# The last down product of each network part taken by pieces of the gated vector, and layer 0's shared network split three to one

## The chip, the cores and the metric

The kernel runs on one core of one Trainium2 chip. The metric is the device time of one execution in microseconds (us), the median of several runs. The five engines are called PE (TensorE), DVE (VectorE), ACT (ScalarE), POOL (GpSimd) and SP (SyncE, which here only issues transfers). Each runs its own queue in order; they wait for one another by semaphores.

## The reference, cut to what matters

Four layers act on x (2 x 1024 tokens of 256 features, float32). Each adds to x a conditioning step followed by a network step:

```python
x = x + _L0_ffn_ref(_L0_cond_ref(x, cond_1024, ...), ...)   # 32 experts, top 1, and a shared network
x = x + _L1_ffn_ref(_L1_cond_ref(x, cond_1024, mask, ...), ...)
x = x + _L2_ffn_ref(_L2_cond_ref(x, cond_1024, ...), ...)   # 8 experts, top 2, and shared networks, twice
x = x + _L3_ffn_ref(_L3_cond_ref(x, cond_1024, ...), ...)   # 8 experts, top 2, shared; then 16 experts with a capacity
```

In the parts that matter here every token goes through a shared gated network and, beside it, through the experts that a router picks:

```python
shared = (silu(x @ gate) * (x @ up)) @ down        # 256 -> 512 -> 256, one or two such units
out    = shared + sum(gates[:, e] * expert_e(x) for the picked e)
```

## The kernel before, in words

**Jobs, pieces, products.** The shared networks are class `Glu`. A job is a pair (unit of weights, chunk of 512 tokens); there are four chunks. The hidden vector of 512 numbers is cut into NF = 4 pieces of 128. `up_part(m)` makes the gate and the up product of piece m % 4 of job m // 4: 12 matmuls of 128x512, as each float32 product is three float32r ones (`matmul_split`, L315 to L322; all matmuls of the shared networks have the lines L320, L321 and L322). ACT takes the silu (L474), DVE multiplies by the up product (`multiply`, L499), ACT copies the high part of the result (`hidden_high`, L481) and DVE subtracts it to give the low part (`hidden_low`, L505), which counts the semaphore `hidden`. `down(n)` then makes the 512x256 result of job n: two halves of 256 tokens, in PSUM banks 6 and 7, each of two groups q of 128 tokens, each group a sum over the four pieces f, so 2 x 2 x 4 x 3 = 48 matmuls of 128x256. It waits once for all four pieces of the job, and for each half until DVE's `add` has taken that bank's previous result. After each half it counts `downed`; `add(n)` takes each half with one DVE instruction (L1498, L1636, L1637 or L1773, by part).

**Order.** `pe_jobs` issues the four up parts of job n + 1, then `down(n)`; for the last job of a call no up parts follow. `dve_jobs` does for each piece m: `multiply(m)`, `hidden_low(m - 1)`, and behind the multiplication of a job's last piece the `add` of the job before and what is given as `between` (`mix`, which adds the gathered expert rows of a chunk; 8 DVE instructions of 128x256 on L1749 or L1882, or one of 128x1024 on L1612 in layer 0). So the `hidden_low` of the very last piece stands behind that `add` and that `mix`.

**Front and behind.** Each of the four network parts (`half_l0`, `half_cond(2)`, `half_ffn2`, `half_cond(3)`) calls `pe_jobs` twice: for the first `split` jobs ahead of the expert stage (the front), with the remaining ones behind it. The fronts cover the routing and the gathering of rows, the part behind covers the loads of the experts' results. Splits are 2 of 4 jobs in layer 0, 4 of 8 in both parts of layer 2, 3 of 4 in layer 3's. At the end PE turns the chunks into feature order (`turn_result`, L447), copied by ACT.

**Layer 0's experts** (`LaneExperts`) run 24 rounds of four lanes. Their weights come through a ring in order of expert, issued by SP (L1051); ACT and DVE copy each round's weights into `own` (L1078), three regions of which lie over the split space of the shared network. `wait_space` says when these are free: the gate weights' region behind all up parts of the front, the up weights' region behind the down product of the job before the front's last.

**Places.** A router's decision becomes row numbers in `Slots`. PE's `pe_places` (L1279 to L1285) waits for a DVE scan (L1272) and is followed on DVE by `places` (L1292 to L1308); only behind this does DVE reach `multiply(0)`. `up_part(3)` and later ones wait until `multiply` has freed the PSUM banks of part m - 3. PE issues up parts 0 and 1 ahead of `pe_places`, 2 and 3 behind it.

Of the kernel before, what the change touches and what calls it, by code (L numbers as in the profile page):

```python
# [23 lines left out]
P = 128  # L24
B, S, D = 2, 1024, 256
T = B * S
NT = T // P
KD = D // P
CH = 512
NCH = T // CH  # L30
TPC = CH // P
TPB = S // P
FU = 512
# [16 lines left out]
def build(nc, a, out):  # L50
    ctx = ExitStack()
    with ctx:
# [263 lines left out]
        def matmul_split(pe, to, w, x, start, stop):  # L316

            pe.matmul(to, w[0], x[0], start=start, stop=False)  # L320
            pe.matmul(to, w[0], x[1], start=False, stop=False)  # L321
            return pe.matmul(to, w[1], x[0], start=False, stop=stop)  # L322
# [56 lines left out]
        class Glu:  # L379
# [42 lines left out]
            def down(self, pe, n):  # L422
# [6 lines left out]
                for half in range(2):  # L429
# [8 lines left out]
                                                f == 0, f == self.NF - 1)  # L438
                    last.then_inc(self.downed, 1)

            def turn_result(self, pe, tok, c, count):

                if count:
                    pe.wait_ge(self.featured, 2 * count)
                for k in range(KD):
                    for q in range(TPC):
                        last = pe.transpose(psum[:, 6 + k, q * P:(q + 1) * P], tok[:, c * TPC + q, k * P:(k + 1) * P], ident[:])  # L447
                    last.then_inc(self.turned, 1)
                self.await_featured = 2 * (count + 1)
# [63 lines left out]
            def pe_jobs(self, pe, n0, n1, first=True, between=None, places=None):  # L513

                if first:
                    for f in range(self.NF):
                        self.up_part(pe, self.NF * n0 + f)
                for n in range(n0, n1):
                    for f in range(self.NF if n + 1 < n1 else 0):
                        self.up_part(pe, self.NF * (n + 1) + f)  # L520
                        if f == 1 and between is not None and n > n0:
                            between(n - 1)
                        if f == 2 and places is not None and n == n0:
                            places.pe_trace(pe)
                    if places is not None and n == n0:
                        places.wait_rows(pe)
                    self.down(pe, n)

            def act_jobs(self, act, n0, n1, between=None):

# [484 lines left out]
        class LaneExperts:  # L1015


            def __init__(self, tag, on, halves, lanes, weights, region_up, region_down, space, rows, slots, glu, hT):

                self.halves, self.lanes, self.weights, self.rows, self.rounds = halves, lanes, weights, rows, rows.tiles  # L1020
                self.tile_expert, self.last_round = slots.tile_expert, slots.last_tile
                self.NE, self.NF, self.F, self.W = weights.shape[0], halves * FU // P, halves * FU, P // lanes
                self.KF, self.FD = KD * self.F, self.NF * D
                self.ring_up = region_up.rearrange("p (r n) -> p r n", r=lanes)
                self.ring_down = region_down.rearrange("p (r n) -> p r n", r=lanes)
                self.own = [space[:, n * lanes * self.KF:(n + 1) * lanes * self.KF].rearrange("p (g n) -> p g n", g=lanes)
                            for n in range(3)]
                self.sg, self.h, self.hT = glu.sg, glu.product, hT
                self.rT = sb(tag + "_rT", [P, 2, KD, P], on=on)
                self.up_in = [sem(f"{tag}_up_in{r}") for r in range(2)]  # L1030
                self.down_in = [sem(f"{tag}_down_in{r}") for r in range(2)]
                self.act_own = [sem(f"{tag}_act_own{n}") for n in range(3)]
                self.dve_own = [sem(f"{tag}_dve_own{n}") for n in range(3)]
                self.rows_t, self.rows_c, self.gate, self.silud, self.up = (
                    sem(f"{tag}_{n}") for n in ("rows_t", "rows_c", "gate", "silud", "up"))
                self.hidden, self.hid_t, self.hid_c, self.downed, self.outc = (
                    sem(f"{tag}_{n}") for n in ("hidden", "hid_t", "hid_c", "downed", "outc"))
# [449 lines left out]
        def half_l0():  # L1487


            with ExitStack() as own:  # L1490
                jobs, split = [(0, 0), (0, 1), (0, 2), (0, 3)], 2
                order, written, scaled, mixed = (sem("h0_" + n) for n in ("order", "written", "scaled", "mixed"))
                got = [sem(f"h0_got{c}") for c in range(NCH)]

# [17 lines left out]
                with nc.Block() as block:  # L1512
                    @block.sync
                    def _(sp):
                        def ready(sp):
                            for c in range(NCH):
                                sp.wait_ge(scaled, c + 1)
                                sp.dma_start(chunk_of(by_token, c), ctok[:, c * TPC:(c + 1) * TPC, :]).then_inc(written, 16)
                            places.wait_known(sp)
                            sp.wait_ge(written, 16 * NCH)  # L1520
                        experts.load_weights(sp, ready)
                        line.wait_stored(sp)
                        for c in (2, 3, 0, 1):
                            load_results(sp, [ctok], c, got[c])
                        sp.dma_start(l1_weights, a["l1_w"]).then_inc(l1_in, 16)
                        sp.dma_start(l1_words[:, 0:TPB, :], a["mask_words"].rearrange("(i p) s -> p i s", p=P)
                                     ).then_inc(l1_mask, 16)
                        sp.dma_start(l1_words[:, TPB, :], a["mask_words"][0, :].partition_broadcast(P)).then_inc(l1_mask, 16)
                        sp.wait_ge(glu.wsplit, 6)
                        sp.dma_start(wbuf[:], unit_data["g2a"]).then_inc(unit_in["g2a"], 16)  # L1530
# [13 lines left out]
                    @block.tensor  # L1544
                    def _(pe):
                        route.pe_logits(pe)
                        route.pe_turn(pe)
                        for m in range(2):
                            glu.up_part(pe, m)
                        places.pe_places(pe)  # L1550
                        for m in range(2, 4):
                            glu.up_part(pe, m)
                        glu.pe_jobs(pe, 0, split, first=False, places=places)
                        pe.wait_ge(glu.added, 2 * split)
                        experts.pe_tiles(pe)
                        glu.pe_jobs(pe, split, NCH)
                        for count, c in enumerate((2, 3, 0, 1)):
                            pe.wait_ge(glu.added, 2 * NCH)
                            pe.wait_ge(mixed, count + 1)
                            glu.turn_result(pe, xtok, c, count)  # L1560

                    @block.scalar
                    def _(act):
                        glu.features_high(act, 0)
                        for q in range(4):
                            glu.weights_high(act, 0, q)
                        route.act_quads(act)
                        for q in range(4, 6):
                            glu.weights_high(act, 0, q)
                        route.act_score(act)  # L1570
                        glu.act_jobs(act, 0, split)
                        places.wait_known(act)
                        first = experts.act_open(act, wait_space)
                        act.wait_ge(glu.downed, 2 * split)
                        experts.act_tiles(act, first)
                        act.wait_ge(experts.hidden, experts.rounds)
                        act.wait_ge(experts.downed, experts.rounds)
                        glu.features_high(act, split)
                        glu.act_jobs(act, split, NCH)
                        for count, c in enumerate((2, 3, 0, 1)):  # L1580
                            glu.copy_result(act, fx, c, count)

                    @block.vector
                    def _(dve):
# [29 lines left out]
                            dve.wait_ge(mixed, count + 1)  # L1614

                        glu.dve_jobs(dve, split, NCH, lambda n: mix(jobs[n][1], n - split))
                        mix(0, 2)
                        mix(1, 3)

        def half_cond(n, wr, bias, units, jobs, split, experts_w, scale, after):  # L1620

# [139 lines left out]
        def half_ffn2():  # L1761


            with ExitStack() as own:
# [22 lines left out]
                with nc.Block() as block:  # L1787
# [23 lines left out]
                    def _(pe):  # L1811
                        route.pe_logits(pe)
                        route.pe_turn(pe)
                        for m in range(2):
                            glu.up_part(pe, m)
                        places.pe_places(pe)
                        for m in range(2, 4):
                            glu.up_part(pe, m)
                        glu.pe_jobs(pe, 0, split, first=False, places=places)
                        pe.wait_ge(glu.added, 2 * split)  # L1820
                        experts.pe_tiles(pe)
# [1309 lines left out]
```

## Time and profile before

| | us |
|---|---|
| median of 3 runs (1671.03 to 1673.64) | 1671.27 |
| the profiled execution, its own time | 1685.24 |
| span of its instructions | 1683.5 |
| PE busy | 1471.8 |
| DVE busy | 984.0 |
| ACT busy | 656.8 |
| POOL busy | 428.6 |

The mean granted TensorE clock of the execution is 0.931 of full speed. The profiled execution took 14.0 us longer than the median of the runs. Times in rows are from the span's start. A timeline row ends with the idle time ahead of it and what released it.

### The profile page before, as it was taken

To read this page: it belongs to the slowest core of one execution; us is meant where nothing else is said; L and a number is where in the kernel's file an instruction comes from. 1 tells how busy PE (TensorE), PEld (TensorE's weight loads), DVE (VectorE), ACT (ScalarE), POOL (GpSimd) and SP (SyncE) were. 2 spreads that over 40 slices of the span, in tenths; PEclk is the share of its full clock that TensorE was granted. 3 is DMA by queue.
4 is the path that set the end of the run, shared out by engine and by line. 5 is a ranking of instruction groups with operands and counts; after the bars stand their busy time and mean duration, and the time that the engine had idled before them with its cause. 6 is when DMAs were issued, how large, how long until landed. Compare 5 with 4: busy or idle time off the path is not lost. (4 is left out here: it accounts for less than half of the span.)

```text
span 1683.5 us, 25908 instructions
## 1 busy us (share of the span) xinstructions
PE 1471.8 (87%) x8350; PEld 1117.3 (66%) x8350; DVE 984.0 (58%) x1754; ACT 656.8 (39%) x977; POOL 428.6 (25%) x366
## 2 busy tenths in 40 slices
PE   7886888765989998798999999999979899759994
PEld 5632334733877787687888888887867777636663
DVE  5665676335644364735777776775646333447665
ACT  3366775213233332424655555553332233211110
POOL 0612231000433410010233443332004334113331
PEclk9999999955899999999999999999998999859997
DMA  5378972252222240240221322201313222355743
GB/s 178 110 289 323 335 250 100 99 195 101 88 100 88 92 153 1 88 175 4 98 101 31 113 86 104 100 23 33 121 33 117 101 86 91 119 209 166 251 147 122
DMA packets 82918, 211.38 MB, mean 126 GB/s; under 512 B 10785, under 2 KB 57762, under 8 KB 74594
## 3 DMA queue, kind: packets, MB, share of 16 engines
q1 hardware_dynamic: 66944, 166.40, 27.6%
q0 software_dynamic: 15840, 43.27, 7.7%
q8 instruction: 76, 1.25, 0.3%
q14 instruction: 56, 0.46, 0.1%
q10 hardware_dynamic: 2, 0.00, 0.0%
HBM read 165.21 MB, written 44.43 MB: 125 GB/s over the span
## 5 line engine op out<-in xcount | busy, mean ns | idle before, releaser
L633 POOL DMA_INDIRECT results<-sb_big,sb_s_out_row x63 | 134.2, 2130 | 452.8 <-ACT sb_big L864 298.1
L938 DVE TENSOR_TENSOR sb_h_split<-sb_big,sb_h_split 128x2048 fp32r<-128x2048 f32 x78 | 178.5, 2289 | 87.1 <-ACT sb_h_split L933 87.1
L933 ACT CAST sb_h_split<-sb_big 128x2048 fp32r x78 | 146.6, 1903 | 34.2 <-issue 32.9
L829 PE MATMUL ps<-sb_big,sb_e_hT 128*128 x624 | 141.0, 379 | 1.1 <-DVE sb_e_hT L986 1.1
L1078 ACT COPY sb_g_space<-sb_big 128x1024 f32 x120 | 118.7, 1050 | 47.5 <-DMA sb_big<-in_l_routed 23.5
L320 PE MATMUL ps<-sb_h_split 128*128 128x512 f32 x312 | 133.1, 426 | 3.8 <-issue 2.8
L1078 DVE COPY sb_g_space<-sb_big 128x1024 f32 x168 | 108.1, 698 | 47.3 <-DMA sb_big<-in_l_routed 21.8
L829 PEld LDWEIGHTS ps<-sb_big,sb_e_hT 128*128 128x128 f32 x624 | 118.2, 190 | 18.5 <-issue 1.3
L1479 POOL DMA_INDIRECT sorted_in<-sb_big,sb_p_slots x64 | 70.2, 1097 | 222.7 <-DVE sb_p_slots L1304 167.4
L322 PE MATMUL ps<-sb_h_split 128*128 128x512 f32 x312 | 123.9, 397 | 0.0
L321 PE MATMUL ps<-sb_h_split 128*128 128x512 f32 x312 | 123.6, 396 | 0.0
L320 PE MATMUL ps<-sb_g_split,sb_g_ws 128*128 128x512 f32 x256 | 107.0, 418 | 13.0 <-DVE sb_g_product L499 8.0
L595 POOL DMA_INDIRECT results<-sb_big,sb_p_out_row x78 | 76.6, 982 | 139.6 <-DVE sb_big L744 139.0
L1116 PE MATMUL ps<-sb_g_space,sb_e_rT 128*32 128x512 f32 x768 | 94.9, 611 | 19.4 <-issue 11.3
L321 PE MATMUL ps<-sb_g_split,sb_g_ws 128*128 128x512 f32 x256 | 104.0, 406 | 0.3 <-issue 0.3
L322 PE MATMUL ps<-sb_g_split,sb_g_ws 128*128 128x512 f32 x256 | 103.4, 404 | 0.0
L622 POOL DMA_INDIRECT sb_big<-by_token,sb_s_in_row x63 | 63.6, 1010 | 145.8 <-DVE sb_s_out_row L1352 127.2
L320 PE MATMUL ps<-sb_g_ws,sb_g_split 128*128 128x256 f32 x256 | 77.4, 303 | 22.9 <-DVE sb_g_split L505 21.3
L474 ACT ACTIVATE sb_g_sg<-ps 128x512 f32<-128x512 f32 x64 | 38.1, 597 | 145.6 <-PE ps L322 136.2
L676 PE MATMUL ps<-sb_big,sb_x_rT 128*128 x312 | 87.5, 403 | 4.2 <-ACT sb_x_rT L721 4.0
L499 DVE TENSOR_TENSOR sb_g_product<-sb_g_sg,ps 128x512 f32<-128x512 f32 x64 | 43.8, 685 | 67.5 <-ACT sb_g_sg L474 59.1
L696 PE MATMUL ps<-sb_big,sb_x_hT 128*128 x312 | 81.8, 385 | 0.0
(450 smaller groups left out, 3193.3 us busy)
## 6 DMA issues: line engine op xcount, KB each, us to landing
sb_big<-in_l_routed SPq DMA_DIRECT2D x32, 1024.0 KB
sb_big<-in_l2f_routed SPq DMA_DIRECT2D x8, 3072.0 KB, 10.6
sb_e_wring<-in_l_experts SPq DMA_DIRECT2D x16, 1408.0 KB
sb_big<-in_l_routed SPq DMA_DIRECT2D x32, 512.0 KB
sb_big<-results SPq DMA_DIRECT2D x32, 512.0 KB, 7.5
sb_big<-sorted_in SPq DMA_DIRECT2D x18, 512.0 KB
by_token<-sb_big SPq DMA_DIRECT2D x12, 512.0 KB, 4.2
sorted_in<-sb_l1p_zero SPq DMA_DIRECT2D x2, 2048.0 KB, 9.6
```

Of the source, the lines that this page charges most:

```text
L320: pe.matmul(to, w[0], x[0], start=start, stop=False)
L321: pe.matmul(to, w[0], x[1], start=False, stop=False)
L322: return pe.matmul(to, w[1], x[0], start=False, stop=stop)
L595: pool.indirect_dma_start(out=results, out_offset=bass.IndirectOffsetOnAxis(ap=places.out_row[:, j:j + 1], axis=0), in_=self.tile(j), in_o ...
L633: pool.indirect_dma_start(out=results, out_offset=bass.IndirectOffsetOnAxis(ap=places.out_row[:, j:j + 1], axis=0), in_=self.tile(j), in_o ...
L676: last = pe.matmul(psum[:, j % 2, 0:self.NF * P], self.rT[:, j % 2, k * P:(k + 1) * P], self.w[:, e, k * self.NF * P:(k + 1) * self.NF * P ...
L696: last = pe.matmul(psum[:, 2 + j % 2, 0:D], self.hT[:, j % 2, f * P:(f + 1) * P], self.w[:, e, lo:lo + D].rearrange("p s n -> p (s n)"), s ...
L829: last = pe.matmul(psum[:, 7, 0:D], self.hT[:, f // TPC, f % TPC * P:(f % TPC + 1) * P], self.weight(place, 2 * KD * self.F + f * D, D), s ...
L933: act.copy(self.own[part][:, 0, :], self.raw(e, part)).then_inc(self.own_high[part], 1)
L938: dve.tensor_tensor(self.own[part][:, 1, :], self.raw(e, part), self.own[part][:, 0, :], ALU.subtract).then_inc(self.own_low[part], 1)
L1078: last = copy(self.own[part][:, g, :], here.rearrange("p s n -> p (s n)"))
L1116: last = pe.matmul(psum[g * W:(g + 1) * W, 2 * part + u % 2, :], self.rT[:, r % 2, k, g * W:(g + 1) * W], self.own[part][:, g, lo:lo + FU] ...
```

## The change

The last job of each call of `pe_jobs` uses a new function in which the pieces f are the outer loop: the product for all four groups of 128 tokens is made for piece 0, then for piece 1, and so on, each waiting for its own piece only; both banks must have been taken by `add` at the start. In layer 0 the split is 3 instead of 2, with the chunks' order behind the experts and the regions of `own` changed to match. In `half_ffn2` alone `pe_places` stands behind three up parts instead of two.

```diff
+            def down_by_hidden(self, pe, n):
+                unit = self.jobs[n][0]
+                if n == 0 or self.jobs[n - 1][0] != unit:
+                    pe.wait_ge(self.wsplit, 6 * unit + 6)
+                if self.await_featured:
+                    pe.wait_ge(self.featured, self.await_featured)
+                if n >= 1:
+                    pe.wait_ge(self.added, 2 * n)
+                for f in range(self.NF):
+                    pe.wait_ge(self.hidden, self.NF * n + f + 1)
+                    for half in range(2):
+                        for q in range(2):
+                            t0, lo = (2 * half + q) * P, 2 * KD * FU + f * D
+                            last = matmul_split(pe, psum[:, 6 + half, q * D:(q + 1) * D],
+                                                [self.hs[:, n % 2, part, f, t0:t0 + P] for part in range(2)],
+                                                [self.ws[:, part, lo:lo + D] for part in range(2)],
+                                                f == 0 and q == 0, f == self.NF - 1 and q == 1)
+                        if f == self.NF - 1:
+                            last.then_inc(self.downed, 1)
@@ pe_jobs
-                    self.down(pe, n)
+                    if n + 1 == n1:
+                        self.down_by_hidden(pe, n)
+                    else:
+                        self.down(pe, n)
@@ LaneExperts
-                            for n in range(3)]
+                            for n in (0, 2, 1)]
@@ half_l0
-                jobs, split = [(0, 0), (0, 1), (0, 2), (0, 3)], 2
+                jobs, split = [(0, c) for c in range(NCH)], 3
+                chunk_order = tuple(range(split, NCH)) + tuple(range(split))
-                        for c in (2, 3, 0, 1):
+                        for c in chunk_order:
                             load_results(sp, [ctok], c, got[c])
-                        for count, c in enumerate((2, 3, 0, 1)):
+                        for count, c in enumerate(chunk_order):
-                        mix(0, 2)
-                        mix(1, 3)
+                        for c in range(split):
+                            mix(c, NCH - split + c)
@@ half_ffn2, tensor
-                        for m in range(2):
+                        for m in range(3):
                             glu.up_part(pe, m)
                         places.pe_places(pe)
-                        for m in range(2, 4):
-                            glu.up_part(pe, m)
+                        glu.up_part(pe, 3)
```

## Rows read from the trace of the kernel before

**Rows 1.** The page: busy time, share of the span and instructions of each engine.

```profile
PE 1471.8 (87%) x8350; PEld 1117.3 (66%) x8350; DVE 984.0 (58%) x1754; ACT 656.8 (39%) x977; POOL 428.6 (25%) x366
```

**Rows 2.** PE's timeline, first matmul of a last down: start, duration, [idle before <-releaser].

```profile
78.66 0.58 PE L320 MATMUL ps<-sb_g_ws,sb_g_split 128*128 128x256 f32 x1 [5.52 <-DVE sb_g_split L505]
314.78 0.58 PE L320 MATMUL ps<-sb_g_ws,sb_g_split 128*128 128x256 f32 x1 [2.64 <-DVE sb_g_split L505]
494.27 0.39 PE L320 MATMUL ps<-sb_g_ws,sb_g_split 128*128 128x256 f32 x1 [1.38 <-DVE sb_g_split L505]
664.01 0.58 PE L320 MATMUL ps<-sb_g_ws,sb_g_split 128*128 128x256 f32 x1 [4.80 <-DVE sb_g_split L505]
1455.76 0.58 PE L320 MATMUL ps<-sb_g_ws,sb_g_split 128*128 128x256 f32 x1 [5.50 <-DVE sb_g_split L505]
```

**Rows 3.** Stretches (last downs): us, busy (x) of PE, PEld, DVE, ACT, POOL, PEclk, DMA, GB/s.

```profile
79.04:82.24 3.20, 3.20 (x16) 3.20 (x16) 2.21 (x4) 0.37 (x1) 0.00 (x0) 0.50 0.02 5
494.27:500.29 6.02, 6.01 (x48) 5.81 (x48) 0.69 (x1) 0.00 (x0) 0.00 (x0) 1.00 0.54 178
664.01:672.27 8.26, 8.26 (x48) 8.26 (x48) 0.69 (x1) 0.00 (x0) 0.00 (x0) 0.65 0.00 0
1243.67:1250.96 7.29, 7.29 (x48) 7.08 (x48) 0.69 (x1) 0.00 (x0) 0.00 (x0) 0.80 0.00 0
1455.76:1464.33 8.57, 8.56 (x48) 8.36 (x48) 0.69 (x1) 0.00 (x0) 0.00 (x0) 0.66 0.02 7
```

**Rows 4.** Timeline of DVE, end of layer 2's conditioning part.

```profile
659.25 0.69 DVE L1637 SCALAR_TENSOR_TENSOR sb_big<-ps,sb_big 128x512 f32<-128x512 f32 x1 [2.18 <-PE ps L322]
659.86 3.37 DVE L1749 SCALAR_TENSOR_TENSOR sb_big<-sb_big,sb_t_gates 128x256 f32<-128x256 f32 x8
663.26 0.69 DVE L505 TENSOR_TENSOR sb_g_split<-sb_g_product,sb_g_split 128x512 fp32r<-128x512 f32 x1
```

**Rows 5.** Timeline of DVE, the front of layer 2's conditioning part.

```profile
492.92 0.69 DVE L1636 TENSOR_SCALAR sb_big<-ps 128x512 f32<-128x512 f32 x1 [2.18 <-PE ps L322]
```

**Rows 6.** Timeline of DVE, layer 3's network part behind its experts.

```profile
1451.53 0.68 DVE L505 TENSOR_TENSOR sb_g_split<-sb_g_product,sb_g_split 128x512 fp32r<-128x512 f32 x1
1455.01 0.69 DVE L505 TENSOR_TENSOR sb_g_split<-sb_g_product,sb_g_split 128x512 fp32r<-128x512 f32 x1
```

**Rows 7.** Timeline of DVE and PE, the end of `half_ffn2`'s front.

```profile
768.88 1.28 DVE L1773 SCALAR_TENSOR_TENSOR sb_big<-ps,sb_big 128x512 f32<-128x512 f32 x2
770.21 0.44 PE L946 MATMUL ps<-sb_ident,sb_big 128*128 128x128 f32 x2 [1.55 <-DVE sb_big L1773]
```

**Rows 8.** Timeline of PE and DVE, the front of layer 0.

```profile
72.86 0.28 PE L322 MATMUL ps<-sb_g_ws,sb_g_split 128*128 128x256 f32 x1
77.31 0.69 DVE L1498 TENSOR_TENSOR sb_big<-ps,sb_big 128x512 f32<-128x512 f32 x1 [6.32 <-remote]
87.18 0.44 PE L1100 MATMUL ps<-sb_ident,sb_big 128*128 128x128 f32 x2 [0.78 <-DVE sb_big L1498]
```

**Rows 9.** Stretches: four up parts (`half_ffn2`); layer 0's network behind its experts.

```profile
744.44:755.35 10.91, 10.91 (x51) 9.02 (x49) 4.56 (x7) 3.32 (x6) 0.00 (x0) 1.00 0.01 2
282.74:323.05 40.31, 36.89 (x193) 32.23 (x193) 16.63 (x24) 8.96 (x16) 0.00 (x0) 0.92 0.44 160
```

**Rows 10.** Stretches: layer 0's first rounds, behind its experts, layer 3's last down.

```profile
88.00:92.00 4.00, 3.86 (x34) 1.04 (x34) 1.30 (x2) 1.39 (x4) 0.00 (x0) 1.00 0.03 10
304.00:308.00 4.00, 4.00 (x26) 3.61 (x25) 2.23 (x4) 2.14 (x5) 0.00 (x0) 1.00 0.00 0
1456.00:1460.00 4.00, 4.00 (x20) 4.00 (x21) 0.00 (x0) 0.00 (x0) 0.00 (x0) 0.50 0.02 6
```

**Rows 11.** PE's timeline about the places of `half_ffn2`.

```profile
689.08 0.39 PE L1279 MATMUL ps<-sb_r_work,sb_ones 128*128 128x8 f32 x2 [1.34 <-DVE sb_r_work L1272]
698.45 0.47 PE L320 MATMUL ps<-sb_h_split,sb_h_ws 128*128 128x512 f32 x1 [1.74 <-DVE sb_h_product L499]
```

**Rows 12.** PE's timeline, layer 0's first expert round.

```profile
88.14 1.92 PE L1116 MATMUL ps<-sb_g_space,sb_e_rT 128*32 128x512 f32 x16 [0.52 <-ACT sb_e_rT L1170]
```

More of the change, by code:

```diff
@@ L1579, in _ @@
                         glu.act_jobs(act, split, NCH)
-                        for count, c in enumerate((2, 3, 0, 1)):
+                        for count, c in enumerate(chunk_order):
                             glu.copy_result(act, fx, c, count)
```

## The prediction

> **What bounds the kernel now.** First the busy times on the page: PE is busy for 1471.8 us, DVE for 984.0 [rows 1], so PE is the engine to read and its idle 212 us are what can go without less arithmetic. Then PE's timeline, looked through for idle time above 1.2 us. All eight last down products have it, always released by L505, the low part of the last piece: 5.52 and 2.64 us in layer 0, 1.38 in the front of layer 2's conditioning part (the fronts of `half_ffn2` and layer 3 repeat this to 0.13 us), 4.80 behind its experts (`half_ffn2` repeats it, 4.79), 5.50 in layer 3 [rows 2]. Together 27.5 us. Then the granted clock over these products: behind 1.38 us of idleness 48 matmuls took 6.02 us at clock 1.00 (the 2.4 GHz level); behind 4.8 us they took 8.26 and 7.29 us at 0.65 and 0.80, behind 5.50 us 8.57 us at 0.66 [rows 3]. So a wait is paid for twice, as idle time and as a product part of which runs at the lower level (1.2 GHz). Last DVE's order: in layer 2 the add of the job before starts at 659.25, the mix takes 3.37 us, and only then comes L505 [rows 4].
>
> **Waits after the change.** The new product needs only both adds to begin; its pieces 0 to 2 are long ready. 36 of 48 matmuls are 36/48 x 6.02 = 4.5 us, and the last 12 take 1.5. From DVE's end to PE's start is 0.06 us (663.26 + 0.69 to 664.01) [rows 2, 4]. The four extra semaphore waits I cost at nothing, as they are fulfilled when PE comes to them; were each 0.06 us it would be 0.2 us a product, 2 in all.
>
> *Layer 2 behind the experts of the conditioning part.* The add ends at 659.94, PE starts at 660.00 instead of 664.01. The mix and L505 end at 663.95, ahead of piece 3 at 664.5, so nothing waits: 4.01 us. The gap left is about 0.8 us, less than the 1.38 that left the clock at 1.00 [rows 2, 3], so I take 6.02 for the product instead of 8.26: 2.24 more. Bounds of this clock term 0 and 2.24. Sum -6.25.
>
> *`half_ffn2` behind its experts.* Same mechanism, same 3.4 us of mix: -4.0 and -(7.29 - 6.02) = -1.27 [rows 3]. Sum -5.27.
>
> *Fronts of the conditioning parts.* No mix stands there, only L505: the add at 492.92 ends at 493.61, PE can start at 493.67 instead of 494.27 [rows 2, 5]: -0.60 each, -1.20 for two.
>
> *Front of `half_ffn2`.* Again 0.6 us earlier, but PE's next instruction waits for the last adds, which on DVE stand behind the copies of the first experts' weights: they run from 768.88 to 770.16 while the down product is over at 768.66, and PE starts at 770.21 [rows 7]. 0; bounds 0 and -0.6.
>
> *Layer 3 behind its experts.* Only one job is there, so no add holds PE. Pieces 0 and 1 follow the up parts at about 1450.3 and last 3.0 us; piece 2's low part is ready at 1452.21, before they end; piece 3's at 1455.70 [rows 6]. PE idles some 1 us, starts the last 12 at 1455.76 and ends at 1457.3 instead of 1464.33 [rows 3]: -7.0. The results for the mixes that follow must have landed: transfers are over by 1456 [rows 10], the next mix starts at 1458. If the clock still fell in the 1 us gap, the last 12 would take 2.6: +1.1.
>
> **Layer 0.** *Front.* Down(0) has its last matmul at 72.86 [rows 8] and matmul starts are 0.12 us apart (6.02/48 less the tail), so it ends at 72.98. Old: DVE got word of it only at 77.31, released by "remote" [rows 8], a lateness of 4.3 us while POOL's gathers ran; the last down follows at 78.66, the experts start at 87.18. New: job 2's up parts follow down(0) at once and hide the lateness: 10.91 us by the stretch of four up parts [rows 9] to 83.9, down(1) 5.8 to 89.7, add to 90.45, last down 90.5 to 96.5, adds 0.8, experts at 97.3. That is +10.1. *Behind.* Old 40.31 us from the first up part to the first turn [rows 9]. New: four up parts and one down less a wait. The 40.31 are 8 up parts, 5.9, 2.64, 7.49 and 0.8, so the up parts took 23.5; four of them at 10.91 drop out, 12.6 stay; 6.0 and 0.8 follow: 19.4. The mix there is one instruction of 1.2 us, and the low part of piece 3 comes within the 4.5 us of the first three. -20.9. Net -10.8. If the lateness were not in an execution at all, the old front would be at 81.2 and the net -4.8; both are bounds. What hides the moved job's other work: its features, silu, multiply and split run on ACT and DVE beside PE's up parts as for the other jobs; SP's queue loses nothing, POOL's gathers are issued at the same time. SP's weight ring restarts when the copies into `own` are made, about 2.3 us nearer to PE's start than now; the transfers almost stand still from 88 to 92 [rows 10], which hides that; uncovered it would cost 2.3. Behind, the transfers of results, layer 1's weights and mask are over by 304 [rows 10] and layer 1 needs them some 21 us earlier than at 332, at 311: 7 us to spare. The changed order of `own` costs nothing, as each region is free before its copy starts.
>
> **The places of `half_ffn2`.** Here I expect a loss. PE waits 1.34 us for the scan, from 687.74 to 689.08 [rows 11]. The third up part takes 10.91/4 = 2.73, to 690.47, so the places come 1.4 us later. DVE waits for them and then works without a pause to the multiplications for which PE waits at 698.45 [rows 11]; PE's time saved there is idle anyway. +1.4; bounds 0 (if DVE's chain had slack) and +2.7 (a whole part).
>
> **Sum.** -10.8 - 6.25 - 5.27 - 1.20 + 0 - 7.0 + 1.4 = -29.1 against the profiled execution's own 1685.24 (span 1683.5 and 1.7 around it): 1656.1. The runs' median is 14.0 us lower, so some stretches seen here, the lateness perhaps among them, are not in every execution. I take half of the 6.0 between the bounds of layer 0: -26, from 1671.27 to 1645.
>
> **A rule against the change.** In an expert round 16 matmuls go in turn to four quarters of PSUM in 1.92 us at clock 1.00 [rows 10, 12], 0.12 each, so going to and fro costs nothing there. The Trainium skill, TensorE: Matmul & The Clock Gate, section "A second HAM failure mode: psum-queue depth-cycling", says that cycling through banks can leave PE with small pauses between groups, enough for the clock to oscillate; the new product changes bank every 6 matmuls and the old one once. By that rule the last products would all run at the lower level, the third rival below; by the row they would not.
>
> **The rivals.**
> 1. *The clock isn't won and the lateness isn't there.* The waits go, but products stay as slow as in rows 3 and layer 0 gives 4.8. For: the clock may respond to more than the gap just before. Against: the 1.38 us gap left it at 1.00. -26 + 3 + (2.24 + 1.27 + 1.1) = -18, 1653.
> 2. *All of it.* The lateness is in the timed runs too and is hidden: -29, 1642; further waits of that kind vanishing could bring some us more.
> 3. *Slower: the product by pieces runs at half pace.* Starts 0.213 us apart at clock 0.50 (15 in 3.20 us) [rows 3] instead of 0.12: 10.2 us a product instead of 6.0, eight times, two of these microseconds hidden in `half_ffn2`'s front: +32. With -26 it is +6, 1677. It decides from 26/8 = 3.3 us a product, 0.07 a matmul. Against it: the expert rounds.
> 4. *No change: the time comes back.* Layer 0's experts are paced by the weight stream and later copies cost what the front's lateness gives, and behind them and in layer 3 the result transfers, not PE, end last. Layer 0 would give 0 and layer 3 some 2 of 7; with the places at +2.7 and the clock terms at 0 some -9 remain, 1662; less than 3 us is left only if layer 2 loses half as well. Against: the idle transfer engines of rows 10.
>
> **How the numbers follow.** Forecast 0.60 (its own range 1641 to 1650), rival 1 0.17, rival 2 0.11, rival 3 0.05, rival 4 0.07, of which 0.04 end within 0.2%. The range 1637 to 1656 holds the forecast and the first two. 0.2% is 3.3 us, about what a measurement of this kernel can tell from no change. Faster 0.90, same 0.04, slower 0.06.
>
> **What would show it.** Right: no idle time above 1.2 us ahead of the last downs, clock 1.00 in them, the product in layer 3 pausing before its last 12 matmuls only; layer 0's experts starting near 97 and the first turn there some 11 us earlier than 323; in `half_ffn2` L1279 1.4 us later after the second up part and the next parts later by as much. Wrong: last downs longer than 6.2 us; a shorter way through the places; an expert stage in layer 0 longer than the present 193 us; PE waiting for a transfer at the start of layer 1.

## The result, and the profile after

| | before | after |
|---|---|---|
| median (us) | 1672.45 (1671.03 to 1673.74, 4 runs) | 1648.46 (1646.90 to 1651.50, 4 runs) |
| profiled execution, its own time | 1685.24 | 1651.50 |
| span, mean granted clock | 1683.5, 0.931 | 1649.8, 0.934 |

The ratio is 0.9859, with a 95% interval of 0.9841 to 0.9877: 24.0 us faster. The profiled executions differ by 33.7 us, more than the medians; where the difference comes from is told below. In the kernel after, L447 has become L468, L474 L495, L499 L520, L505 L526, L1078 L1102, L1279 L1303, L1498 L1523, L1636 and L1637 L1661 and L1662, L1749 L1774, L2874 L2898.

The page of the kernel after, busy times:

```profile
PE 1462.4 (89%) x8350; PEld 1109.7 (67%) x8350; DVE 983.9 (60%) x1754; ACT 657.0 (40%) x977; POOL 428.0 (26%) x366
```

The same instructions are there as in [rows 1]. PE is busy 9.4 us less, as more of its work runs at the higher level of the clock (mean 0.934 against 0.931), and its idle time in the span falls from 211.7 to 187.4 us.

PE's timeline after, at the last downs, as in [rows 2]: the front and behind in layer 0, the front and behind in layer 2's conditioning part, behind in `half_ffn2`, and in layer 3 the first matmul of the last piece:

```profile
92.60 0.39 PE L320 MATMUL ps<-sb_g_ws,sb_g_split 128*128 128x256 f32 x1 [0.79 <-DVE sb_big L1523]
305.96 0.28 PE L320 MATMUL ps<-sb_g_ws,sb_g_split 128*128 128x256 f32 x1
482.45 0.39 PE L320 MATMUL ps<-sb_g_ws,sb_g_split 128*128 128x256 f32 x1 [0.78 <-DVE sb_big L1661]
648.22 0.36 PE L320 MATMUL ps<-sb_g_ws,sb_g_split 128*128 128x256 f32 x1 [0.83 <-issue]
1222.54 0.35 PE L320 MATMUL ps<-sb_h_ws,sb_h_split 128*128 128x256 f32 x1 [0.83 <-issue]
1423.46 0.39 PE L320 MATMUL ps<-sb_g_ws,sb_g_split 128*128 128x256 f32 x1 [1.19 <-DVE sb_g_split L526]
```

Where a job stands before the last one, 0.78 to 0.83 us of idle time remain. The releaser is now the `add` in the fronts; behind the experts of layer 2 the trace names none ("issue"), but in the conditioning part the `add`, shown below, ends 0.10 us before PE's start. Behind layer 0's experts the job is alone, and PE doesn't pause. The low part L526 releases PE once, in layer 3, 1.19 us ahead of the last 12 matmuls. Windows over these products, to set against [rows 3] (us, busy (x) of PE, PEld, DVE, ACT, POOL, PEclk, DMA, GB/s):

```profile
92.60:98.61 6.01, 6.01 (x48) 5.80 (x48) 3.72 (x6) 1.35 (x2) 0.00 (x0) 1.00 0.12 19
648.22:654.21 5.99, 5.99 (x48) 5.79 (x48) 4.52 (x10) 0.00 (x0) 0.00 (x0) 1.00 0.01 1
1222.54:1228.51 5.97, 5.97 (x48) 5.77 (x48) 4.52 (x10) 0.00 (x0) 0.00 (x0) 1.00 0.00 0
1417.80:1425.16 7.36, 6.17 (x49) 5.76 (x47) 5.39 (x12) 1.73 (x3) 0.00 (x0) 1.00 0.83 264
```

All have clock 1.00 and 0.12 us a matmul. In [rows 3] the first had 0.50 in the stretch shown, the others 0.65, 0.80 and 0.66. DVE, at the end of layer 2's conditioning part, to set against [rows 4]; the mix of L1774 now lies beside PE's product instead of ahead of it:

```profile
647.43 0.69 DVE L1662 SCALAR_TENSOR_TENSOR sb_big<-ps,sb_big 128x512 f32<-128x512 f32 x1 [2.18 <-PE ps L322]
```

**Stage by stage.** Distances in us between landmarks in the traces. "Behind" runs from the first matmul of the last group of expert products to the next stage's first matmul, layer 3's front from the rows' trace (L1338 before) to the first expert product, and the last row from the first expert product to the last. "places" is the kernel before with only the places moved; it and the two others stand here because they ran beside kernels before that took 1672 to 1673 us, near the median, and not 1685 as the profiled execution did.

| stretch | before | places | after | after again (e9) | pieces alone (e10) |
|---|---|---|---|---|---|
| layer 0, start to first expert product | 88.1 | 83.3 | 100.4 | 99.8 | 83.1 |
| its expert products | 188.6 | 189.5 | 186.4 | 188.8 | 185.0 |
| their end to layer 1 | 55.5 | 54.0 | 35.0 | 33.2 | 50.9 |
| sum to layer 1 | 332.2 | 326.8 | 321.8 | 321.8 | 319.0 |
| layer 1 | 72.5 | 72.8 | 73.0 | 72.8 | 71.3 |
| behind, layer 2 conditioning | 83.7 | 82.6 | 77.2 | 77.2 | 77.2 |
| `half_ffn2`, start to places | 11.8 | 14.6 | 13.0 | 14.6 | 11.8 |
| behind, `half_ffn2` | 89.6 | 90.8 | 84.3 | 84.3 | 84.4 |
| front, layer 3 conditioning | 55.2 | 46.5 | 45.9 | 45.9 | 45.9 |
| behind, layer 3 conditioning | 41.7 | 40.6 | 34.9 | 34.8 | 34.9 |
| layer 3's last expert products | 152.2 | 153.7 | 156.8 | 153.6 | 156.7 |

Layer 1 is in the table because no edit touches it: over all fourteen traces it takes from 68.3 us (e6, mean granted clock 0.63) to 73.1 (e11, 0.55). Differences of that size between two single traces can come without any change.

### The profile page after: what moved, and what is told of

Read it like the earlier page. It is cut to its first block and busy times, and to the rows that moved or that the text cites. A ratio compares the mean times of both kernels' runs of the same rounds, so it can differ in the third digit from the quotient of the medians.

```text
span 1649.8 us, 25908 instructions
## 1 busy us (share of the span) xinstructions
PE 1462.4 (89%) x8350; PEld 1109.7 (67%) x8350; DVE 983.9 (60%) x1754; ACT 657.0 (40%) x977; POOL 428.0 (26%) x366
## 5 line engine op out<-in xcount | busy, mean ns | idle before, releaser
L1102 DVE COPY sb_g_space<-sb_big 128x1024 f32 x168 | 107.9, 698 | 48.8 <-DMA sb_big<-in_l_routed 23.2
L1102 ACT COPY sb_g_space<-sb_big 128x1024 f32 x120 | 118.5, 1046 | 40.7 <-DMA sb_big<-in_l_routed 21.7
L495 ACT ACTIVATE sb_g_sg<-ps 128x512 f32<-128x512 f32 x64 | 38.1, 597 | 143.5 <-PE ps L322 143.3
L520 DVE TENSOR_TENSOR sb_g_product<-sb_g_sg,ps 128x512 f32<-128x512 f32 x64 | 43.9, 685 | 74.1 <-ACT sb_g_sg L495 73.1
L2898 PE MATMUL ps<-sb_e_wring,sb_e_rT 128*128 x124 | 66.6, 662 | 11.6 <-issue 5.1
```

What stands on the lines that cost most here:

```text
L1102: last = copy(self.own[part][:, g, :], here.rearrange("p s n -> p (s n)"))
L2898: last = pe.matmul(psum[:, j % 2, :], rT[:, j % 2, k * P:(k + 1) * P], wring[:, place, k * FU:(k + 1) * FU].rearrange("p s n -> p (s n)"), ...
```

## The experiments

The kernels ran in three groups of four, each group beside its own runs of the kernel before. Those had medians of 1671.81 us (first group, 23 runs), 1687.21 (second, 11 runs) and 1673.34 (third, 11 runs), so ratios and not times are compared between groups. The record gives each group a chip of its own, so group and chip can't be told apart here. One run of 23 in the first group's kernel before (1771.07 us) and one of 12 in e3's (3800.73) stand far outside; the medians don't depend on them.

**e1: the product by pieces alone.** The change without its edits of the split and of the places.

```diff
-                jobs, split = [(0, c) for c in range(NCH)], 3
+                jobs, split = [(0, c) for c in range(NCH)], 2
-                        for m in range(3):
+                        for m in range(2):
```

> Only the last down products by pieces, in all four network parts; layer 0 split 2 to 2 and the places as before. Theory (wait and clock, place by place from the two traces): -6.3 in layer 2's conditioning part, -5.3 in its network part, -7.0 in layer 3, -0.6 in each of two fronts, and in layer 0 without the split some -0.6 in front and -3 behind (2.64 us of waiting less 0.8, and a product at full clock): about -23 us. Rival (most of the gain is the layer 0 split, the rest comes back): -12 us or less.

Measured: 1646.30 (1643.30 to 1647.77), ratio 0.9848 [0.9823, 0.9873], 25.5 us less. I expected some 23. The product by pieces brings all that the whole change brought (24.0).

**e2: the split alone.** The split of three to one with the old `down` and the old places.

```diff
-                    if n + 1 == n1:
-                        self.down_by_hidden(pe, n)
-                    else:
-                        self.down(pe, n)
+                    self.down(pe, n)
```

> Only layer 0's split 3 to 1, with its chunk order and its copies' regions; all down products as before. Theory: three jobs in front hide the late word of down(0), but the last downs keep their own wait for L505 (1.4 us in front; behind, with a single job, some 4 us at the lower clock): -10.8 less what the pieces give there, so -3 to -7 us if the lateness is in the timed runs, about 0 if it is a thing of the profiled execution only. Rival (the split alone makes the gain of 10): -10 us.

Measured: 1669.28, ratio 0.9986 [0.9970, 1.0002]: 2.5 us less, which the interval does not tell from nothing. In its trace the part up to layer 1 takes 325.1 us, where "places", which has the old layer 0, has 326.8. The last down behind layer 0's experts still waits for the low part, and runs below full clock (PE's timeline, then a window):

```profile
307.62 0.38 PE L320 MATMUL ps<-sb_g_ws,sb_g_split 128*128 128x256 f32 x1 [3.87 <-DVE sb_g_split L526]
```

```profile
307.62:315.00 7.38, 7.38 (x48) 7.29 (x48) 0.69 (x1) 0.00 (x0) 0.00 (x0) 0.77 0.29 120
```

A job that is alone behind the experts has its mix ahead of its last low part, too: the split moves work, but not the wait.

**e3: the places alone.**

```diff
-                        for m in range(2):
+                        for m in range(3):
                             glu.up_part(pe, m)
                         places.pe_places(pe)
-                        for m in range(2, 4):
-                            glu.up_part(pe, m)
+                        glu.up_part(pe, 3)
```

> Only half_ffn2's places behind three up parts instead of two. Theory: DVE's chain from the scan's count to the multiplications sets the end there, so the part is 1.1 to 1.4 us slower: +1.2 us in all. Rival (PE is the bound and gains the moved part's time): -1 to -3 us.

Measured: 1672.64 (all but one run 1666.35 to 1676.34), ratio 1.0006 [0.9987, 1.0025], not resolved in time. The trace shows the loss where it was looked for: `half_ffn2` reaches the places 14.6 us from its start instead of 11.8, and from there to the rows' trace takes 19.7 in place of 19.8. Three up parts stand ahead of the places (windows over those 36 matmuls, first e3, then the kernel after):

```profile
674.38:684.23 9.85, 9.85 (x36) 8.01 (x37) 5.74 (x18) 4.91 (x6) 0.00 (x0) 0.83 0.25 82
```

```profile
663.69:671.99 8.30, 8.30 (x36) 6.87 (x37) 5.75 (x18) 4.92 (x6) 0.00 (x0) 1.00 0.29 98
```

The same 36 matmuls cost 9.85 us at clock 0.83 and 8.30 at 1.00, and e9, the same kernel as the one after, has 9.90 at 0.83. So the move costs 1.2 us or 2.8, as the clock happens to be.

**e4: the change with the old places.** The kernel after, with `range(2)` and the two remaining up parts behind the places.

```diff
-                        for m in range(3):
+                        for m in range(2):
```

> The changed kernel with half_ffn2's places back behind two up parts. Theory: 1.2 us faster than the changed kernel, so some 25 us below the kernel before. Rival (the third up part belongs ahead of the places): 1 to 3 us slower than the changed kernel.

Measured: 1646.78 (1642.03 to 1651.25), ratio 0.9850 [0.9823, 0.9876]. It is beside e1 (0.5 us apart), so with the pieces in, three to one and two to two are the same there. Against the kernel after (0.9859, another group) a gain from the old places of 1 to 3 us is not excluded and not shown by the times.

**e5: keep PE busy in the gaps.** The kernel before, with matmuls whose results nobody reads in the gaps behind the experts. Nothing ends earlier on DVE.

```diff
+                self.warm = {'g0': 20, 'g2': 36, 'h2': 36, 'g3': 40}[tag]
+                if warm:
+                    m = self.NF * (n + 1) - 2
+                    pe.wait_ge(self.multiplied, m + 1)
+                    for _ in range(warm):
+                        pe.matmul(psum[:, m % 3 * 2, 0:D], self.ws[:, 0, 0:P], self.ws[:, 0, 0:D], start=True, stop=True)
```

> The kernel before with matmuls of no use (20, 36, 36 and 40, each 128x256, result thrown away in a free PSUM bank) in PE's wait ahead of the last down product behind the experts, in layer 0, both parts of layer 2, and layer 3. Waits stay as they are; only the idleness goes. Theory (a gap costs twice, the product behind it runs partly at 1.2 GHz): the four products take 6.0 us instead of 7.5, 8.3, 7.3 and 8.6, so -7 us. Rival (the lower clock comes from something other than the gap): products as long as before, 0 or slightly slower.

Measured: 1672.84 beside 1687.21, ratio 0.9916 [0.9886, 0.9946], 14.4 us less (9 to 19). Windows over the four products behind the experts:

```profile
314.30:320.33 6.03, 6.01 (x48) 5.81 (x48) 0.69 (x1) 0.00 (x0) 0.00 (x0) 1.00 0.00 0
661.70:667.70 6.00, 5.98 (x48) 5.77 (x48) 0.69 (x1) 0.00 (x0) 0.00 (x0) 1.00 0.01 3
1238.80:1244.80 6.00, 5.95 (x48) 5.82 (x48) 0.69 (x1) 0.00 (x0) 0.00 (x0) 1.00 0.01 3
1449.60:1455.60 6.00, 5.97 (x48) 5.81 (x48) 0.69 (x1) 0.00 (x0) 0.00 (x0) 1.00 0.04 15
```

The real matmuls are the same and wait for the same low part as before, and they take 6.0 us instead of 7.5, 8.5, 7.3 and 8.6 (the second from its start to the end of its last matmul, 0.24 us more than the stretch in [rows 3]):

```profile
664.01:672.51 8.50, 8.50 (x48) 8.30 (x48) 0.69 (x1) 0.00 (x0) 0.00 (x0) 0.66 0.00 0
```

So the idle stretch itself lowered the clock, and that is worth 7.8 us by these four alone, where 7 were expected. The stretches of the table that hold them (to layer 1, and the three behind) are shorter than before's by 1.9, 2.5, 1.3 and 2.6 us, 8.3 in sum, and the two profiled executions differ by as much (1685.24 and 1676.72). The medians differ by 14.4, and by 9 at the least; what is above 8.3 isn't placed.

**e6: the low part first.** The kernel before with one DVE instruction moved: the low part of a call's very last piece is made ahead of the `add` and the mix. The product stays whole.

```diff
+                    if m == self.NF * n1 - 1:
+                        self.hidden_low(dve, m)
@@ behind the loop
-                self.hidden_low(dve, self.NF * n1 - 1)
```

> The kernel before with one change on DVE: the low part of the last piece (L505) right behind the piece's multiplication, ahead of the add of the job before and of the mix; products in the old order. Theory (DVE's order made the wait, the order of the product only hides it): PE goes from one down product to the next without a wait in layer 2 and the fronts, and waits some 2.7 us in layer 3; -25 us in all, as much as the pieces give. Rival (the pieces themselves are needed): -8 us or less.

Measured: 1657.51 beside 1687.21, ratio 0.9829 [0.9798, 0.9859], 29.7 us less, where I expected 25: as much as the product by pieces (0.9848 and 0.9853). DVE's timeline behind layer 2's conditioning part: two low parts together, then the two adds, then the first of the mix:

```profile
641.59 1.46 DVE L505 TENSOR_TENSOR sb_g_split<-sb_g_product,sb_g_split 128x512 fp32r<-128x512 f32 x2
643.23 0.69 DVE L1638 SCALAR_TENSOR_TENSOR sb_big<-ps,sb_big 128x512 f32<-128x512 f32 x1 [0.18 <-PE ps L322]
646.11 0.69 DVE L1638 SCALAR_TENSOR_TENSOR sb_big<-ps,sb_big 128x512 f32<-128x512 f32 x1 [2.19 <-PE ps L322]
646.72 0.47 DVE L1750 SCALAR_TENSOR_TENSOR sb_big<-sb_big,sb_t_gates 128x256 f32<-128x256 f32 x1
```

PE has no idle time at all ahead of this last down. In layer 0's front 2.06 us remain, released by the `add`. A wait for the low part is left only where a job is alone, in layer 3, since the up parts end 2.8 us ahead of it:

```profile
1426.93 0.39 PE L320 MATMUL ps<-sb_g_ws,sb_g_split 128*128 128x256 f32 x1 [2.79 <-DVE sb_g_split L505]
```

The product behind this pause runs at full clock all the same (window over it):

```profile
1426.93:1432.95 6.02, 6.01 (x48) 5.81 (x48) 3.36 (x9) 0.00 (x0) 0.00 (x0) 1.00 0.51 160
```

The waits of [rows 2] thus came from DVE's order, and either side can take them away: PE asks for less at a time, or DVE does the awaited part first.

**e7 and e8: both together, split two and three.** Low part first, and the product half by half with piece 3 last; a job that is alone goes piece by piece. e8 has layer 0's three to one, both have the old places. The core of e7, then what e8 changes (with it the regions of `own`, as in the change):

```diff
+                order = [(f, half) for half in range(2) for f in range(self.NF - 1)]
+                if alone:
+                    order = sorted(order)
+                seen = set()
+                for f, half in order + [(self.NF - 1, 0), (self.NF - 1, 1)]:
+                    if f == 0 and n >= 1:
+                        pe.wait_ge(self.added, 2 * (n - 1) + half + 1)
...
-                jobs, split = [(0, c) for c in range(NCH)], 2
+                jobs, split = [(0, c) for c in range(NCH)], 3
```

> Layer 0 split 2 to 2, places as before, the last down by pieces, and two things more: its pieces 0 to 2 are made half by half, so that the first half waits for its own bank's add only, and DVE makes the last low part ahead of add and mix. Theory: the remaining waits of 0.8 us (four of them) and the 1.2 us in layer 3 go: 4 us faster than the product by pieces alone, -29 us against the kernel before. Rival (these waits are hidden behind DVE, whose add and mix still have to follow): as the pieces alone, -25 us.

> As e7_halves_low, with layer 0's split of 3 to 1. Theory from the first four runs (with the pieces the split is worth about nothing): within 1 us of e7_halves_low. Rival (three jobs in front still help by the wait behind the experts): 2 us faster than it.

Measured: e7 1658.46, ratio 0.9833 [0.9803, 0.9864]; e8 1651.16, ratio 0.9797 [0.9767, 0.9826]. Beside e6 (0.9829) e7 shows no gain at all, where 4 us over the pieces alone were expected: with a split of two to two, both edits together give no more than either. In their traces e7 is 2.0 us shorter than e6 up to layer 1 and 2.8 behind in layer 3's conditioning part, but 4.5 longer in layer 1, which has the same code in both.

Three to one took 7.3 us more off the median, where I expected at most 1. The traces differ by as much (spans 1656.7 and 1649.4), but hardly where the edit is: up to layer 1 e7 takes 323.5 us and e8 323.0. Of the rest 1.9 lie in layer 1 and 2.6 behind layer 3's conditioning part, the others in pieces of under 1, all in equal code. In both, `add` in a front gets word of PE late, as in [rows 8]. DVE's timeline of e8:

```profile
468.20 0.69 DVE L1670 TENSOR_SCALAR sb_big<-ps 128x512 f32<-128x512 f32 x1 [5.07 <-remote]
```

**e9 to e12: the four against one another.** All beside a kernel before of 1673.34. e9 is the change again, e10 is e1's code, e11 is e8's. e12 is e8 with the plain product:

```diff
-                    if n + 1 == n1:
-                        self.down_by_hidden(pe, n, n == n0)
-                    else:
-                        self.down(pe, n)
+                    self.down(pe, n)
```

> The changed kernel again, beside the others on one chip, to see how its gain differs by chip. Theory (the late words of down products are a property of the chip, and layer 0's split is worth 6 us only where they come): on a chip where the kernel before takes some 1687 us it is 30 us faster, where that takes 1671 us 24 us. Rival (the difference was spread of the runs): 24 to 27 us on either.

> The product by pieces alone again (as e1_pieces). Theory: on a chip with late words 5 to 7 us slower than the changed kernel, on one without within 1 us of it (1.2 us of the places against it). Rival: the same on both.

> e8_halves_low_split again, beside the changed kernel: pieces half by half, the last low part ahead of add and mix, split 3 to 1, places as before. Theory: 0.8 us at four places, 1.2 us in layer 3 and 1.2 us of the places: 5 us faster than the changed kernel. Rival: DVE's work only moves behind the product, no more than 2 us.

> As e11_best with the last down in its old order, all four sums one after the other: only DVE's order, the split of 3 to 1, and the old places. Theory (the pieces have nothing left to hide but 2.7 us of silu, product and split where a part has one job, in layers 0 and 3): 4 to 6 us slower than e11_best. Rival (pieces needed everywhere): 15 us slower.

| | median | ratio |
|---|---|---|
| e9, the change | 1650.24 (1648.86 to 1651.72) | 0.9864 [0.9837, 0.9891] |
| e10, pieces alone | 1649.02 (1640.17 to 1652.82) | 0.9853 [0.9820, 0.9885] |
| e11, low part first, pieces, three to one | 1638.07 (1635.45 to 1640.47) | 0.9788 [0.9761, 0.9816] |
| e12, low part first, three to one | 1645.82 | 0.9841 [0.9812, 0.9870] |

e9 gains 23.1 us, near the 24 expected where the kernel before takes 1671, and e10 lies within 1.2 us of it, as expected there too; no kernel after ran in the second group, so the 30 expected there were not tested. e11 is the fastest: 12.2 us less than the change, without overlap of their runs. I expected 5. PE's timeline of e11 at the end of layer 2's conditioning part and of layer 3's: behind the start of the last up part the first idle time stands ahead of `turn_result`, none ahead of or within the last downs.

```profile
650.60 1.10 PE L476 MATMUL ps<-sb_ident,sb_big 128*128 128x128 f32 x8 [0.78 <-DVE sb_big L1671]
1418.15 1.09 PE L476 MATMUL ps<-sb_ident,sb_big 128*128 128x128 f32 x8 [1.13 <-DVE sb_big L1671]
```

By the table's stretches e11 is shorter than e9 by 2.6 us up to layer 1, by 1.06 behind in layer 2's conditioning part, 1.06 behind in `half_ffn2`, 1.0 and 1.06 in layer 3's front and behind, 2.7 at the places, and 2.4 in layer 2's front, which varies by 1 or more between executions of equal code. Each 1.06 is the 0.8 us for the last `add` that e9's product waits for, and a little. e12 is 7.8 us slower than e11, where 4 to 6 were expected. It differs by the waits of lone jobs: 3.0 us behind in layer 0 and 4.2 in layer 3, where this row stands instead of e11's seamless product:

```profile
1414.59 0.39 PE L320 MATMUL ps<-sb_g_ws,sb_g_split 128*128 128x256 f32 x1 [2.79 <-DVE sb_g_split L534]
```

Both pauses of e12 last 2.8 us, but only the one in layer 3 has a slow product behind it (windows over the two products, layer 0 and layer 3):

```profile
304.04:310.05 6.01, 6.01 (x48) 5.80 (x48) 1.77 (x2) 0.00 (x0) 0.00 (x0) 1.00 0.54 227
1414.59:1422.09 7.50, 7.50 (x48) 7.30 (x48) 3.36 (x9) 0.00 (x0) 0.00 (x0) 0.77 0.42 133
```

## Why the prediction was right, and where its terms were not

Forecast 1645, measured 1648.5: the forecast case held, at the slow end of its own range. From 1671.27, as in the text, the change took 22.8 us where -26 was said.

**Waits and clock.** Right in every place. PE starts 0.8 us behind the down product of the job before, the clock is 1.00, and the products take 5.97 to 6.01 us where 6.02 was taken. The stretch behind layer 2's conditioning part lost 6.5 us (predicted 6.25; with the old product at its full 8.50 us instead of 8.26 the same sum gives 6.49), that behind `half_ffn2` 5.3 in both executions (5.27), layer 3's 6.8 (7.0, with 1.19 us ahead of the last 12 matmuls where "some 1 us" stood). Against "places", whose products have other clocks (0.79, 0.67 and 0.78 where before has 0.66, 0.80 and 0.66), they are 5.4, 6.5 and 5.7. So the waits are certain, while the clock's part of each term is that of one execution. e5 shows the clock term by itself, which rival 1 had at nothing: that half of it falls, while its other half (no lateness in the timed runs) holds in layer 0, below. The front of `half_ffn2` gave 0, as said: DVE's adds end at 752.95 and release PE at 753.01, and from the rows' trace to there both kernels take 61.3 us.

**Pieces at half pace.** Rival 3 is refuted by the windows: changing banks every 6 matmuls costs nothing, 0.12 us a matmul. By the Trainium skill, TensorE: Matmul & The Clock Gate, section "A second HAM failure mode: psum-queue depth-cycling", products that cycle through banks can let the clock oscillate; this case's traces don't agree (6.01, 5.99 and 5.97 us at 1.00).

**Layer 0.** The step that was mis-sized. The term was -10.8, bounds -4.8 to -10.8, and half of the 6.0 between them was taken. The profiled executions show -10.4, as the late word in [rows 8] was there before and is gone after: DVE gets word of down(0) on time, at 75.20, and layer 0's experts and first turn come at 99.39 and 312.65 (predicted 97.3 and 312; in this execution PE reaches down(0) 2.0 us later than in the one of before, at 69.24 and not 67.23, and the expert products take 2.2 less):

```profile
75.20 0.69 DVE L1523 TENSOR_TENSOR sb_big<-ps,sb_big 128x512 f32<-128x512 f32 x1 [2.19 <-PE ps L322]
```

```profile
99.39 0.44 PE L1124 MATMUL ps<-sb_ident,sb_big 128*128 128x128 f32 x2 [0.79 <-DVE sb_big L1523]
312.65 0.44 PE L468 MATMUL ps<-sb_ident,sb_big 128*128 128x128 f32 x2 [0.78 <-DVE sb_big L1523]
```

But in the groups where the kernel before takes 1672 and 1673 us no trace has such lateness ("places": 83.3 us to the first expert product and not 88.1), and there layer 0 gave 5.0 us (326.8 to 321.8 in two executions), the lower bound; e4, with the same layer 0, has 319.9, or 6.9 us. And the reason given for the larger number, that job 2's work in front hides something, is not borne out: pieces alone get layer 1 started at 319.0 and 321.9 us (e10, e1), the change at 321.8. The split is worth nothing measurable in the first and third groups. What gave time in layer 0 was the product by pieces. The 7.8 us in the forecast were a middle between two bounds and not a reading: by the execution the term is 5.0, 6.9 or 10.4. With 5.0 in its place the forecast's sum is 23.3 us and its time 1648, so this term can be all that the forecast was off by.

**Places.** Sign right, size +1.4 against +1.2 and +2.8 measured, the upper bound being +2.7. That both sizes occur was missed: I priced the third up part at full clock only.

**Not forecast.** Two stretches. Layer 3's front took 55.2 us in the profile of before and 45.9 after. The old trace has PE pausing between matmuls of one product, which the new one has not (PE's timeline, before):

```profile
1312.55 0.38 PE L320 MATMUL ps<-sb_g_ws,sb_g_split 128*128 128x256 f32 x1 [1.02 <-issue]
1314.67 0.28 PE L322 MATMUL ps<-sb_g_ws,sb_g_split 128*128 128x256 f32 x1 [1.63 <-issue]
```

All traces in which `add` gets late word have 53.3 to 55.2 us there, all others 44.9 to 46.5, whatever the edit. The 9 us are thus a property of the execution, not the change. They and the lateness in layer 0 (5.4 us) are in the profiled executions' 33.7 us and, by these traces, not in the medians' 24.0; the stretch below, 4.6 us longer after, makes up for part of them. The waits by releaser show the late words (before: engine, line, releaser: us in total, times, longest), and the kernel after has no row of this kind:

```profile
DVE sb_big L1636 <- remote: 11.8, 3, 5.1
DVE sb_big L1498 <- remote: 6.3, 1, 6.3
DVE sb_big L1773 <- remote: 5.1, 1, 5.1
ACT sb_g_space L1078 <- remote: 4.9, 1, 4.9
```

The second stretch is layer 3's last experts: 156.8 us after 152.2. PE's timeline before, then after, at its wait for expert weights:

```profile
1562.66 2.48 PE L2874 MATMUL ps<-sb_e_wring,sb_e_rT 128*128 x4 [2.38 <-DMA sb_e_wring<-in_l_experts]
```

```profile
1528.43 2.40 PE L2898 MATMUL ps<-sb_e_wring,sb_e_rT 128*128 x4 [3.16 <-DMA sb_e_wring<-in_l_experts]
```

This is rival 4's mechanism (time given back to a transfer), but e9, the same kernel, has 153.6, and e1 155.2. Over all traces this stretch has 152.2 to 156.8: the four kernels that kept their waits (before, e2, e3, e5) have 152.8 on the mean, the ten others 154.7. Some 2 us may be given back, and single executions don't tell them from spread.

**What stays open.** Why the same pause of 2.8 us left the clock high twice and not the third time was not tested. What makes PE's word reach DVE late, and PE pause in the same stretches, in some groups and not in others, was not tested. It goes with the group and with none of the edits: every trace of the second group has it, though the edits of three of them took away waits that the first group kept. As each group had its own chip, it may be the chip: the record has no chip in two groups, and doesn't say where the first executions ran. Nor is there a cause for e8's 7 us over e7. If the three to one split hides late words, as I argued for layer 0, that would be it, but the one execution of each that was traced shows 0.5 us there.

## What to carry to other kernels

Where PE waits for the last piece of something, look first at what stands ahead of that piece on the producing engine: moving one instruction gave as much here (0.983) as rebuilding the product (0.985). Both together gave no more (0.983) with layer 0 split two to two, and most (0.979 and 0.980) with three to one; why the split counts only there is open. Price such a wait twice, as idle time and as the following matmuls at the lower clock level, but take the second price for a bound: pauses of 2.8 us cost 1.5 us again in one place and nothing in two. And before a stretch of a single trace is counted as gain, compare it with traces of the same code in other executions: some 9 of the 34 us by which these two profiles differ have nothing to do with the change, and layer 1, which nobody touched, varies by 4.8.

## What the runs showed of the hardware

- The clock behind a pause of PE: 0.8 to 1.4 us of idleness left 48 matmuls at 5.97 to 6.02 us and 1.00. In the traces of before, e2 and e3, 2.6 and 3.9 us went with 7.3 to 7.5 us, 4.8 with 7.3 to 8.5, 5.5 with 7.4 to 8.6. But 2.8 us went with 6.0 us and 1.00 in e6 and in e12's layer 0, and with 7.5 us and 0.77 in e12's layer 3. Matmuls without use in the pause, down to an idle 0.2 to 0.7 us, gave 6.0 us again (e5).
- The same kernel before took 1672, 1687 and 1673 us in three groups of runs. The slower group is the one whose traces show late words and 53 to 55 us in layer 3's front.
- Three up parts ahead of the places ran at clock 1.00 in one execution of the kernel after and at 0.83 in the other, 8.30 against 9.90 us, with the same matmuls and the same pauses ahead (0.98, 1.71 and 0.45 us in both). The pause just ahead does not settle the level by itself.
- Layer 1, with the same code in all kernels, took 68.3 us at a mean granted clock of 0.63 in one execution and 73.0 at 0.55 in another.
